# Convolution slots of a graph network: both fp32 products first, and a new order at the end of the first LSTM pass

## The reference

```python
h = relu(einsum('ts,bsh->bth', adj, x @ Wg0 + bg0))
h = relu(einsum('ts,bsh->bth', adj, h @ Wg1 + bg1))
for p in range(1, MAX_SKIP + 1):          # MAX_SKIP = 4
    nw = Tv // p
    wins = h[:, :nw * p, :].reshape(Bv * nw, p, Hd)
    last = lstm_last(Wih[p - 1], Whh[p - 1], bih[p - 1], bhh[p - 1], wins)
    h = h.at[:, arange(nw) * p + (p - 1), :].set(last.reshape(Bv, nw, Hd))
```

## Time and profile before

| | |
|---|---|
| time, median of 3 runs | 889.64 us (889.62 to 889.95) |
| span of the profiled execution | 888.1 us |
| PE busy | 862.1 us (97%) |
| DVE busy | 702.2 us (79%) |
| ACT busy | 606.4 us (68%) |
| POOL busy | 237.2 us (27%) |
| granted TensorE clock, mean | 0.993 |
| share of PE on the chain that ended last | 60% |

### The profile page before, as it was taken

One profiled execution on the slowest core, in us unless ns is written; L12 is line 12 of the kernel. 1 busy time (PEld: TensorE's weight loads), 2 busy tenths in 40 slices (PEclk: granted clock), 3 DMA queues, 4 the chain that ended last, 5 costly groups with the idle time before them and its releaser, 6 DMA issues.

```text
span 888.1 us, 15204 instructions
## 1 busy us (share of the span) xinstructions
PE 862.1 (97%) x5228; PEld 744.1 (84%) x5228; DVE 702.2 (79%) x1572; ACT 606.4 (68%) x1117; POOL 237.2 (27%) x562
## 2 busy tenths in 40 slices
PE   8999999989999999999999999999998999999996
PEld 7888888868778788999998887878887898888885
DVE  5888888858888868777777777677987887887886
ACT  3877777767667776767676666666886777776354
POOL 0233333430000000000000001003564565556765
PEclk9999999999999999999999999999999999999998
DMA  4221121000000001000000076766173011111123
GB/s 142 68 60 60 62 60 47 1 1 1 1 1 0 1 1 48 1 1 1 1 2 0 18 173 154 160 161 142 48 167 72 14 37 37 37 37 37 49 61 83
DMA packets 30987, 45.43 MB, mean 51 GB/s; under 512 B 2592, under 2 KB 23744, under 8 KB 27840
## 3 DMA queue, kind: packets, MB, share of 16 engines
q1 hardware_dynamic: 27680, 27.34, 10.4%
q0 software_dynamic: 2304, 16.78, 9.3%
q10 hardware_dynamic: 928, 0.35, 0.2%
HBM read 19.29 MB, written 8.39 MB: 31 GB/s over the span
## 4 chain that ended last, share of the span: by engine, by line
PE 60%; DVE 12%; ACT 4%; issue 3%; POOL 0%; POOLq 0%; DVEq 0%; ACTq 0%
PE psum L504 7%; PE psum L505 7%; PE psum L506 7%; PE psum L1259 6%; PE psum L1335 6%; PE psum L522 5%; PE psum L518 5%; PE psum L519 5%; PE psum L1348 2%; PE psum L1315 2%; ACT work L646 2%; PE psum L1286 2%; DVE work L966 2%; PE psum L1251 2%; DVE work L984 2%
## 5 line engine op out<-in xcount | busy, mean ns | idle before, releaser
L646 ACT ACTIVATE work<-psum,bias 128x512 f32<-128x512 f32 (+1 forms) x408 | 232.0, 623 | 26.5 <-PE psum L522 25.5
L504 PE MATMUL psum<-hT_hi,w_hi 128*128 128x512 f32 (+1 forms) x406 | 148.4, 365 | 3.7 <-ACT work L646 2.6
L505 PE MATMUL psum<-hT_lo,w_hi 128*128 128x512 f32 (+1 forms) x406 | 146.5, 361 | 0.0
L506 PE MATMUL psum<-hT_hi,w_lo 128*128 128x512 f32 (+1 forms) x406 | 146.4, 360 | 0.0
L630 ACT ACTIVATE work<-work 128x512 f32<-128x512 f32 (+1 forms) x112 | 63.9, 571 | 108.2 <-DVE work L973 71.9
L984 DVE TENSOR_TENSOR work<-work 128x512 f32<-128x512 f32 (+1 forms) x111 | 68.0, 612 | 54.0 <-ACT work L630 54.0
L518 PE MATMUL psum<-hs_hi,w_hi 128*128 128x512 f32 (+1 forms) x288 | 103.9, 361 | 1.2 <-DVE hs_hi L918 1.0
L522 PE MATMUL psum<-hs_lo,w_hi 128*128 128x512 f32 (+1 forms) x288 | 104.6, 363 | 0.0
L519 PE MATMUL psum<-hs_hi,w_lo 128*128 128x512 f32 (+1 forms) x288 | 103.1, 358 | 0.0
L1167 POOL DMA_DIRECT2D hT_lo<-hT_hi x8 | 7.5, 935 | 352.8 <-DVE hT_lo L920 332.6
L504 PEld LDWEIGHTS psum<-hT_hi,w_hi 128*128 128x128 f32 x406 | 76.5, 188 | 18.2 <-ACT work L646 4.9
(11 more groups left out here) (225 smaller groups left out, 1911.4 us busy)
## 6 DMA issues: line engine op xcount, KB each, us to landing
work<-x_by_batch SPq DMA_DIRECT2D x32, 256.0 KB, 2.6
x_stage<-x_by_state SPq DMA_DIRECT2D x8, 1024.0 KB, 5.3
hT_lo<-hT_hi POOLq DMA_DIRECT2D x8, 1024.0 KB, 9.9
hT_lo<-x_stage POOLq DMA_DIRECT2D x8, 1024.0 KB, 7.2
out<-x_kept SPq DMA_DIRECT2D x31, 256.0 KB, 2.3
work<-L_gnn_Wih SPq DMA_DIRECT2D x4, 256.0 KB, 3.0
work<-L_gnn_Whh SPq DMA_DIRECT2D x3, 256.0 KB, 3.0
out<-x_kept SPq DMA_DIRECT2D x2, 128.0 KB, 2.3
```

The lines of the kernel that those rows point to most:

```text
L504: pe.matmul(out, w_hi[:, w, g, :], xh, start=True, stop=False)
L505: pe.matmul(out, w_hi[:, w, g, :], xl, start=False, stop=False)
L506: mm = pe.matmul(out, w_lo[:, w, g, :], xh, start=False, stop=(t == 0))
L646: op = act.activation(gate[s][g][:, 0:ph.width], psum[:, 4 * s + g, 0:ph.width], ACT.Tanh if g == G else ACT.Sigmoid, bias=bias[:, b:b + 1])
```

## The change

TensorE's slot is cut into functions and gets a new order: feature product of tile n, second neighbour product of tile n-2, gate I, neighbour product, gate G, gate O, second feature product. The two fp32 groups stand side by side, and the five split groups follow.

`first_input` moves from slot 36 to slot 34 (`FIRST_INPUT = tiles + 2`), between gate O of tile 29 and the second feature product of tile 31, so two gates of the second pass are ready before the last two tiles of the first pass. They count on a semaphore of their own, `first_gates`, and ScalarE's waits for gates I and G of later steps are one lower. VectorE's `seed` comes ahead of the cell product in the last slots (it differs from before in slot 34 alone, since no later slot has both).

```diff
+    FIRST_INPUT = tiles + 2
-            pe.matmul(out, w_lo[:, w, g, :], xh, start=False, stop=True).then_inc(gate_psum[g], 1)
+            pe.matmul(out, w_lo[:, w, g, :], xh, start=False, stop=True).then_inc(S["first_gates"], 1)
...
         def slot(n):
             if has(n):
+                features(n)
+            if has(n - 2):
+                second_neighbours(n - 2)
             if has(n - 5):
...
                 gate_product(I, n - 5)
             if has(n - 1):
+                neighbours(n - 1)
             if has(n - 5):
                 gate_product(G, n - 5)
+                gate_product(O, n - 5)
+            if n == FIRST_INPUT:
                 first_input(I, XW, S["xw_ready"])
                 first_input(G, AH, S["ahT_ready"])
             if has(n - 3):
+                second_features(n - 3)
...
-                        act.wait_ge(gate_psum[g], nf if g == F else n + 1)
+                        if ph is phases[1] and it == 0 and k == 0 and g != O:
+                            act.wait_ge(S["first_gates"], 1 + (g == G))
+                        else:
+                            act.wait_ge(gate_psum[g], nf if g == F else n + 1 if g == O else n)
...
+            if has(n - 4) and has(n - 3):
+                seed(n - 3)
             if ended and has(n - 5):
                 cell_product(n - 5)
-            if has(n - 4) and has(n - 3):
-                seed(n - 3)
```

More of the change, by code:

```diff
@@ L114, in front @@
     BACK_WEIGHTS = 7
+    FIRST_INPUT = tiles + 2
+    assert FIRST_INPUT > piece_slot[-1]
     SORT_COLS, SORT_ROWS, ADJACENT = 8, 12, 16
@@ L195, in front @@
              "xw_psum xw_hi xw_ready h1_psum h1_ready ah_psum ahT_hi ahT_ready h2_psum h2_hi h2_done first_sum seeded "
-             "gates_read f_ready ig_ready tanh_ready fc_done ig_done c_ready h_mul h_hi first_hi h_done tiles_done "
+             "first_gates gates_read f_ready ig_ready tanh_ready fc_done ig_done c_ready h_mul h_hi first_hi h_done tiles_done "
              "rows_loaded cols_loaded a_loaded iota_done a_zero tables_f ecol_done key_done spreads ranks permutes rows_psum rows_ready cols_psum cols_ready "
@@ L400, in first_input, with features @@
             pe.matmul(out, w_hi[:, w, g, :], xl, start=False, stop=False)
-            pe.matmul(out, w_lo[:, w, g, :], xh, start=False, stop=True).then_inc(gate_psum[g], 1)
+            pe.matmul(out, w_lo[:, w, g, :], xh, start=False, stop=True).then_inc(S["first_gates"], 1)
+        def features(n):
+            pe.wait_ge(x_loaded[n % X_RING], 16 * (n // X_RING + 1))
+            if n:
+                pe.wait_ge(S["xw_ready"], n)
+            else:
+                pe.wait_ge(S["wg0_loaded"], 16)
+            for b in range(BT):
+                mm = pe.matmul(psum[:, XW, b * P:(b + 1) * P], x_tile[n % X_RING][:, b, :], wg0[:, :], start=True, stop=True)
+            mm.then_inc(S["xw_psum"], 1)
@@ new lines, in neighbours @@
+        def neighbours(k):
+            if k:
+                pe.wait_ge(S["h1_ready"], k)
+            else:
+                pe.wait_ge(S["adjT_ready"], 3)
+            pe.wait_ge(S["xw_ready"], k + 1)
+            out = psum[:, H1, :]
+            pe.matmul(out, adjT_hi[:, :], xw_hi[:, k % 2], start=True, stop=False)
+            pe.matmul(out, adjT_lo[:, :], xw_hi[:, k % 2], start=False, stop=False)
+            pe.matmul(out, adjT_hi[:, :], xw_lo[:, k % 2], start=False, stop=True).then_inc(S["h1_psum"], 1)
@@ new lines, in second_neighbours, with second_features @@
+        def second_neighbours(k):
+            pe.wait_ge(S["h1_ready"], k + 1)
+            if k:
+                pe.wait_ge(S["ahT_ready"], k)
+            for b in range(BT):
+                mm = pe.matmul(by_batch(psum[:, AH, :])[:, b, :], h1[k % 2][:, b, :], adjT[:, :], start=True, stop=True)
+            mm.then_inc(S["ah_psum"], 1)
+        def second_features(k):
+            if not k:
+                pe.wait_ge(S["wg1_ready"], 1)
+            out, cols = psum[:, H2, :], block_of(k)
+            pe.wait_ge(S["ahT_ready"], k + 1)
+            pe.wait_ge(S["seeded"], k + 1)
+            pe.matmul(out, wg1_hi[:, :], hT_hi[:, cols], start=False, stop=False, skip_group_check=True)
+            pe.matmul(out, wg1_hi[:, :], hT_lo[:, cols], start=False, stop=False, skip_group_check=True)
+            pe.matmul(out, wg1_lo[:, :], hT_hi[:, cols], start=False, stop=True, skip_group_check=True).then_inc(S["h2_psum"], 1)
@@ L419, in slot @@
             if has(n - 1):
[L420 to L429, removed]
+                neighbours(n - 1)
             if has(n - 5):
                 gate_product(G, n - 5)
[L432 to L440, removed]
+                gate_product(O, n - 5)
+            if n == FIRST_INPUT:
                 first_input(I, XW, S["xw_ready"])
                 first_input(G, AH, S["ahT_ready"])
-            if has(n - 5):
-                gate_product(O, n - 5)
             if has(n - 3):
[L446 to L454, removed]
+                second_features(n - 3)
         def first_sum():
```

## The result

The changed kernel took 893.85 us (median of 4 runs, 893.05 to 894.88) against 889.64 us for the kernel before: 1.005 times as long, with a 95% interval of 1.0038 to 1.0062. One more run of the kernel before, of 1046.42 us, was in a slow state and is left out. The changed kernel is slower, by 4.2 us; the forecast was 892.9 us, 3.3 us slower.

What follows compares the result with a forecast made beforehand. TensorE's own work bounds full slots, the chain through other engines the last slots. Losses of 0.51 + 0.52 + 4.2 + 0.26 = 5.5 us less a 2.2 gain give 3.3, so 889.64 + 3.3 = 892.9 us; range 889.0 to 894.8.

Steps and rivals of the forecast that it cites:

- No price for changing formats: Full slots: two fp32 groups side by side save nothing on format changes, 0.00 us a slot (upper bound 0.02).
- The ring: Ordinary full slots: second neighbour product waits on VectorE's bank AH read behind gate G; 5.40 against TensorE's 5.27, 0.13 us lost.
- The group: Slots 11 to 28, three per weight piece: TensorE waits for delayed VectorE, losing 0.70 us six times, 4.2 us.
- The start: Slots 5 and 6: late second neighbour product delays gate I, the table load and the cell product; 0.51 us lost.
- The last slots: Tile 31's feature product to second pass's first gate: path over two cell products held by POOL, gain 2.2 us.
- I let the delay go through to the end: From the second pass on: TensorE's order is as before, so the 3.3 us delay reaches the end unchanged.
- pieces absorbed: Full slots: piece work fits where ScalarE and VectorE wait for gate G, six times 0.44 less, 890.3 us; chance 0.13.
- ordinary slots absorbed: Ordinary full slots: second neighbour product doesn't wait, slots stay at 5.27 us, total 890.6 us; chance 0.11.
- Only one product held: End of first pass: POOL holds one cell product, tile 30's ends 0.9 us earlier, total 892.0 us; chance 0.09.
- The second feature product waits too: Slot after a weight piece: second feature product waits 0.2 us, six times, total 894.1 us; chance 0.09.
- A tail gain without a loss: Whole kernel: full slots lose nothing, only the gain at the first pass's end stays, some 887.4 us; chance 0.10.
- The signs named beforehand: Profile: second neighbour product waiting, 5.4 us ordinary slots, tile 31 near 168.5, no 3 us wait, first gate near 196.

Runs made afterwards that it cites:

- the last slots alone: Changed kernel with the second neighbour product put back between gates G and O, the rest of the change kept; 886.34 us, 0.9972 times the kernel before.

## Why the prediction was right, and where it was not

The sign, the two mechanisms and their places were right. By its own steps:

- **No price for changing formats: right.** 0.89 us from feature product to SN are eight passes; slots with the groups side by side and no ring take 5.28 or 5.29.
- **The ring: right.** 5.42 measured, 5.40 forecast, from links of 3.26, 0.72, 0.61 and 0.83 against 3.25, 0.72, 0.60 and 0.83. With gate G and the reading of bank AH moved forward it is gone.
- **The group: right in mechanism, mis-sized.** Between cell products over a piece slot lie 6.18 us (forecast 6.16); SN to SN took 5.79, 5.80 and 5.42 (forecast 5.79, 5.77 and 5.40). Hundredths in each link made 17.0 in place of 16.96, and the six groups lost 4.44 in place of 4.2: most of what the full slots lost beyond the forecast.
- **The start: right.** From the feature product of tile 5 to SN of slot 6 the forecast has 29.68 - 22.80 = 6.88, and 6.88 was measured (23.67 to 30.55). Slots 5 to 10 lost 1.08 (forecast 0.51 + 0.52).
- **The last slots: right.** Laid out from SN of slot 31 (170.69): cell product of tile 29 over at 19.42 (forecast 19.36), POOL's next subtraction at 21.57 (21.61), cell product of tile 30 over at 23.39 (23.42), first gate at 26.58 (26.60). The gain over the stage is 2.21, forecast 2.2. The experiments show what the forecast could only argue: with POOL's subtractions cut short both products go free.
- **"I let the delay go through to the end": wrong.** That is the step that failed, and its term was 0.52 us in place of 0. Two subtractions that hold two cell products were laid out; the same instruction runs a third time, for tile 31. In the old order it ended 0.23 us into the second pass's first state product, which took 0.78. In the new one h_mul of tile 31 has to wait for POOL (1.27 us) and stands 0.70 us behind the first gate in place of 0.14; the subtraction that follows it starts 2.55 behind that gate in place of 1.59, and holds that state product (1.42). Seven kernels here have one or both edits of the last slots, one state buffer and the subtractions whole and at their place, and all take 25.99 to 26.02 in this stage; the two with the old last slots take 25.50 and 25.51.

In the sum 5.81 - 2.21 + 0.52 - 0.07 = 4.05 us stands against 5.5 - 2.2 = 3.3: 0.3 in the full slots, 0.5 behind the first gate. The two misses go the same way, so neither hides the other. The medians (893.32 and 893.85) differ from the forecast by 0.4 and 0.95, a part of which is the start that moves.

The rivals: *pieces absorbed* and *ordinary slots absorbed* fell with the late SN and the 5.42. *Only one product held* fell with 1.35 and 1.64. *The second feature product waits too* has no row in the list of waits between tiles 5 and 31. *A tail gain without a loss* is not what the change does, but what it can do: from tile 5 on the last slots alone are 2.38 us shorter than before, near that rival's 2.2. They gain 3.13, because the 0.94 that the slot order costs there isn't lost, and give 0.51 back behind the first gate. Their median, 886.34, is a microsecond under the rival's 887.4; the profile started 1.2 us earlier than that of before.

The signs named beforehand came with three reservations. The feature product of tile 31 was expected near 168.5 and the first gate near 196, and both were about 1.2 later, 0.87 of it from the start. The wait of SN is recorded as idle time only in the late slots. And 5.4 us from feature product to feature product holds for ordinary slots outside the groups (5.41 and 5.42 in slots 29 and 30); inside a group the three are 5.86, 5.28 and 5.87, since SN moves within its slot.

## What to carry to other kernels

An order on one engine closes rings through the queues of others: before an instruction is moved ahead, follow its waits round until they come back to it, and compare that sum with the engine's own time for a slot. Here the two were within 3% (5.42 and 5.27), and a piece of work that comes every third slot on other engines made nearly half of the loss (2.7 of 5.8 us). And when a stretch gets shorter, lay out every later run of each instruction that was found holding something, not only those in the stretch: the next one will meet new neighbours.

## What the runs showed of the hardware

VectorE's product of two tiles in memory and POOL's subtraction hardly run side by side, in either order. POOL first: the product ends 0.54 to 0.55 us after POOL, and takes 1.64 to 1.68 in place of 0.69 where it starts 0.13 to 0.18 behind POOL, 1.35 where it starts 0.48 behind. VectorE first, by 0.29: the product takes 0.76 and POOL's subtraction 1.60 in place of 1.28; cut to four columns it takes 0.20 alone and 0.53 behind a product that began 0.29 earlier. The Trainium skill, "SBUF — State Buffer", section "Who interferes with whom", says that such a pair contends and that whoever issues first keeps the other out for its whole instruction. The runs agree on who waits; that the product ends 0.55 and not 0.69 after POOL makes its hold 0.14 shorter than a whole product behind POOL would be.

In the two kernels with a wait of 3.02 us the clock fell right behind it. In the kernel with the slot order alone, busy time by stretch right behind the wait of 3.02 us, with the columns of the earlier trace rows:

```profile
190.70:193.90 3.20, 3.17 (x8) 2.52 (x9) 1.35 (x2) 1.18 (x2) 1.89 (x2) 0.57 0.00 0
```

The granted clock falls from its full level (2.4 GHz) to about the half (1.2 GHz) for these 3 us, as it did in the kernel before (0.50). Busy time by stretch in the kernel with `seed` alone, around the wait of 1.18 us that it leaves:

```profile
176.00:186.00 10.00, 8.16 (x34) 5.77 (x33) 7.49 (x10) 7.01 (x13) 3.89 (x5) 1.00 0.01 2
```

The clock stays at 1.00 there. So it does behind the wait of 1.63 that `first_input` alone leaves (1.00 from 178 to 190), and in the changed kernel, where no such wait is left.
